# A third PSUM bank for the attention's transposes from tile 15 on, and the next step's decision two tiles earlier

## The reference

```
x = x + conv_attention(layernorm_over_channels(x))     # 7x7 local attention
t = tokens(x)                                          # 4 x 1024 x 64
t = t + steps(layernorm(t))
```

```
op = argmax(h[0, 0, :19])
q, k, v = h @ wq[op], h @ wk[op], h @ wv[op]
attn = softmax(q @ k.T / 8);  y = (attn @ v) @ wo[op]     # 1024 x 1024 per image
h = y if attn_mask[op] else h
z = relu(h @ w1[op] + b1[op]) @ w2[op] + b2[op]
h = z if ffn_mask[op] else h
```

## Time and profile before

| | |
|---|---|
| time, median of 3 runs | 262.25 us (262.2 to 262.34) |
| the profiled execution's own time | 261.88 us |
| its span in the trace | 260.0 us |
| TensorE busy (matmuls) | 230.6 us, 89% |
| VectorE busy | 170.7 us, 66% |
| ScalarE busy | 160.2 us, 62% |
| mean granted TensorE clock | 0.954 |

### The profile page before, as it was taken

The page is one execution under the profiler, slowest core; times in us unless marked ns, Lnnn a source line. Parts: engine busy times, 40 slices in busy tenths (PEclk is TensorE's granted clock), DMA queues, the critical chain, the costliest instruction groups (busy, mean ns, idle before and its releaser), DMA issues.

```text
span 260.0 us, 5251 instructions
## 1 busy us (share of the span) xinstructions
PE 230.6 (89%) x1794; PEld 156.5 (60%) x1795; DVE 170.7 (66%) x312; ACT 160.2 (62%) x297; POOL 39.5 (15%) x66
## 2 busy tenths in 40 slices
PE   7879963999999996499869999999999999998992
PEld 3247623787777744233247687887877777777320
DVE  0279937677778736146385999898687666871652
ACT  1928753366666784045456997879877776663541
POOL 9800042454444100700000000000000000000000
PEclk9999997799999996579989999999999999999999
DMA  6850000000000010000100000000000000000006
GB/s 167 186 108 1 4 0 1 0 3 0 0 0 0 0 31 0 10 0 3 43 0 0 3 0 0 3 0 3 0 3 0 3 0 3 0 3 0 0 16 149
DMA packets 3304, 4.80 MB, mean 18 GB/s; under 512 B 1041, under 2 KB 2257, under 8 KB 3282
## 3 DMA queue, kind: packets, MB, share of 16 engines
q1 hardware_dynamic: 2758, 3.86, 6.6%
q10 hardware_dynamic: 524, 0.64, 1.1%
HBM read 3.45 MB, written 1.05 MB: 17 GB/s over the span
## 4 chain that ended last, share of the span: by engine, by line
PE 75%; ACT 9%; DVE 7%; issue 6%; ACTq 2%; POOL 0%; DVEq 0%; POOLq 0%
PE ps L594 11%; PE ps L608 11%; PE ps L582 8%; PE ps L660 7%; PE ps L435 7%; PE ps L674 6%; PE ps L467 5%; PE ps L456 5%; ACT arena L883 4%; PE ps L446 2%; PE ps L410 2%; PE ps L334 2%; PE ps L563 2%; DVE arena L996 2%; PE ps L352 2%
## 5 line engine op out<-in xcount | busy, mean ns | idle before, releaser
L883 ACT COPY arena<-ps 128x1024 f32<-128x1024 f32 x32 | 32.4, 1011 | 20.4 <-PE ps L594 19.4
L582 PE MATMUL ps<-h_st,g_st 128*128 128x512 f32 x128 | 39.5, 431 | 2.6 <-DVE h_st L1094 2.3
L1107 DVE TENSOR_REDUCE negmax<-ps 128x1 f32<-128x1024 f32 x32 | 38.7, 1219 | 3.8 <-PE ps L582 3.6
L832 ACT ACTIVATE pr<-ps,negmax 128x1024 f32<-128x1024 f32 x32 | 35.8, 1119 | 4.0 <-DVE negmax L1107 3.7
L594 PE MATMUL ps<-eye,pr 128*128 128x128 f32 x256 | 33.7, 275 | 2.7 <-ACT arena L883 2.3
L594 PEld LDWEIGHTS ps<-eye,pr 128*128 128x128 f32 x256 | 28.6, 140 | 11.1 <-issue 5.0
L608 PE MATMUL ps<-arena,vk 128*64 128x128 f32 x512 | 31.5, 276 | 1.1 <-ACT arena L883 1.1
L608 PEld LDWEIGHTS ps<-arena,vk 128*64 128x64 f32 x512 | 27.6, 137 | 3.8 <-issue 2.3
L766 ACT ACTIVATE prob<-ps,negmax 128x308 f32<-128x308 f32 x32 | 16.3, 513 | 21.0 <-DVE negmax L1007 21.0
L582 PEld LDWEIGHTS ps<-h_st,g_st 128*128 128x128 f32 x128 | 22.2, 193 | 11.3 <-DVE h_st L1094 3.5
L1117 DVE TENSOR_SCALAR pr<-pr,rinv 128x1024 f32<-128x1024 f32 x32 | 24.1, 753 | 1.1
(11 more groups left out here) (110 smaller groups left out, 335.7 us busy)
## 6 DMA issues: line engine op xcount, KB each, us to landing
arena<-in_key_onehot SPq DMA_DIRECT2D x4, 361.0 KB, 6.2
out<-tabs SPq DMA_DIRECT2D x8, 128.0 KB, 2.3
x<-in_x SPq DMA_DIRECT2D x2, 256.0 KB, 3.9
x<-in_x ACTq DMA_DIRECT2D x2, 256.0 KB, 5.2
w1d<-in_ffn_w SPq DMA_DIRECT2D x4, 64.0 KB, 2.1
w2p<-in_ffn_pack SPq DMA_DIRECT2D x2, 65.5 KB, 1.9
spread_w<-in_spread_mat SPq DMA_DIRECT2D x4, 32.0 KB, 5.0
mean_w<-in_mean_mat SPq DMA_DIRECT2D x1, 96.0 KB, 2.1
```

The source lines that it names most:

```text
L582: mm = nc.tensor.matmul(ps[:, 2 * h + c, :], g_st[:, b2, h, q0:q0 + P], h_st[:, b2, h, part, c * 512:c * 512 + 512], start=(part == 0), st ...
L832: nc.scalar.activation(pr[:, n % 2, :], ps[:, 2 * (n % 2):2 * (n % 2) + 2, :], ACT.Exp, bias=negmax[:, 0, n % 2:n % 2 + 1], accum_out=rows ...
L883: nc.scalar.copy(prt[:, n // 8 % 2, n % 2, :, q0:q0 + P], ps[:, 4:6, :].rearrange("p b (c q) -> p (b c) q", c=4)).then_inc(S["s_pt"], 1)
L1107: nc.vector.tensor_reduce(negmax[:, 0, n % 2:n % 2 + 1], ps[:, 2 * (n % 2):2 * (n % 2) + 2, :], mybir.AxisListType.XY, ALU.max, negate=Tru ...
```

## The change

From tile 15 on (`RING`), an odd tile's transposes go to banks 5 and 6 and begin with bank 6, and an even tile's go to banks 4 and 5 and begin with bank 4. In both cases four transposes are issued before the wait for the copy of the previous tile, and four, into the shared bank 5, behind it. The ScalarE copy reads the two banks in their order. Since bank 6 also carries the row for the decision, `turn_row(6)` is issued at tile 12 and `decide` at tile 13, and `tile_turn(15)` waits for `decided`. Tiles 0 to 14 are transposed as before.

```diff
+RING = 15
...
                 def tile_turn(n):
                     pe.wait_ge(S["s_prob"], base + n + 1)
+                    bank, halves = 4, (0, 1)
                     if n == 0:
                         pe.wait_ge(S["vo_copied"], 3 * a + 1)
-                    else:
+                    elif n < RING:
                         pe.wait_ge(S["s_pt"], base + n)
-                    for c in range(NKC):
-                        mm = nc.tensor.transpose(ps[:, 4 + c // 4, (c % 4) * P:(c % 4) * P + P],
-                                                 pr[:, n % 2, c * P:c * P + P], eye[:])
+                    elif n % 2 == 1:
+                        bank, halves = 5, (1, 0)
+                    if n == RING:
+                        pe.wait_ge(S["decided"], a + f + 2)
+                    for i in halves:
+                        if n >= RING and i == halves[1]:
+                            pe.wait_ge(S["s_pt"], base + n)
+                        for c in range(4 * i, 4 * i + 4):
+                            mm = nc.tensor.transpose(ps[:, bank + i, (c % 4) * P:(c % 4) * P + P],
+                                                     pr[:, n % 2, c * P:c * P + P], eye[:])
                     mm.then_inc(S["s_turned"], 1)
...
-                    if n == 14:
+                    if n == 12:
                         pe.wait_ge(S["vo_copied"], 3 * a + 3)
                         pe.wait_ge(S["h_ready"], chunks + 5)
                         turn_row(6)
...
                     q0 = (n // 2 % 4) * P
+                    bank = 5 if n >= RING and n % 2 == 1 else 4
                     nc.scalar.copy(prt[:, n // 8 % 2, n % 2, :, q0:q0 + P],
-                                   ps[:, 4:6, :].rearrange("p b (c q) -> p (b c) q", c=4)
+                                   ps[:, bank:bank + 2, :].rearrange("p b (c q) -> p (b c) q", c=4)
                                    ).then_inc(S["s_pt"], 1)
...
-                           11: lambda: store(0), 15: lambda: decide(a + f + 1, 6, ev),
+                           11: lambda: store(0), 13: lambda: decide(a + f + 1, 6, ev),
```

## The result

The changed kernel took 258.73 us (median of 6 runs, 256.8 to 259.27) beside 261.88 us for the kernel before (6 runs, the three shown ahead among them); the ratio is 0.987 with a 95% interval of 0.9828 to 0.9912. In a second comparison the two came to 258.63 and 261.56 us, ratio 0.9907 (0.9878 to 0.9936). So it is about 3 us faster. The forecast was 258.9 us with a range of 258.3 to 260.3.

A forecast was written before the change was run, and what follows sets the result against it. TensorE's exposed waits for ScalarE's copy were taken to lie on the path; -3.6 for eight waits, +0.2 for late weight loads and +0.1 for a store made -3.3, from 262.25 to 258.9 us, range 258.3 to 260.3.

The forecast's parts named there:

- The bound: Attention tiles: TensorE's transposes wait for ScalarE's copy nine times, 2.3 us idle, on the path to the end.
- The waits that go: Odd tiles from 15 to 29: eight exposed waits for the copy vanish, 0.45 us each, 3.6 us together.
- The wait in the middle: Between an odd tile's fourth and fifth transposes: met by 0.02 us; late weight loads cost 0.2 us in all.
- What is late next: VectorE and ScalarE beside TensorE's 5.71 us pairs: their loop does not bind; a store costs 0.1 us.
- the loop over VectorE and ScalarE: Exponentials, normalising, maxima and copy of a tile pair: 5.51 us, 0.20 under TensorE's 5.71, so not binding.
- The 0.1 us for `store(1)`: VectorE's store after tile 19 delays tile 20's normalising: 0.1 us, bounds 0 and 0.3.
- The decision and its row: Row's transpose moved from tile 14 to 12, `decide` now earlier on VectorE: net 0, bounds -0.1 and +0.1.
- The sum: Whole kernel: -3.6 + 0.2 + 0.1 = -3.3 us, giving 258.9 us from the median of 262.25 us.
- A: Wait inside a run breaks overlap of weight loads; eight odd tiles pay 0.16 us each; 260.1 us; chance 0.16.
- B: VectorE and ScalarE become the bound, pairs of 5.9 us, gain only 2.1 us; 260.2 us; chance 0.10.
- C: Wait inside the run costs a full restart in all 17 tiles from 15 to 31; 262.9 us; chance 0.04.
- D: Second half still waits for the whole copy, early transposes only fill idle time; 262.2 us; chance 0.04.

The follow-up runs named there:

- e1: Kernel before with only the row's transpose moved to tile 12 and the decision to tile 13: stretch 64.38 us, median 261.58 us, ratio 0.9959.
- e4: Changed kernel with the wait for the previous tile's copy put ahead of the first four transposes: stretch 64.31 us, median 261.24 us, ratio 0.9962 to before.
- e5: Changed kernel plus one single-column ScalarE copy ahead of each even tile's copy from 16 on: stretch 61.00 us, median 258.08 us, ratio 0.9873 to before.
- e5b: Changed kernel plus two single-column ScalarE copies ahead of each even tile's copy from 16 on: stretch 61.66 us, median 258.92 us, ratio 0.9901 to before.
- e7: Changed kernel plus a VectorE memset ahead of each even tile's maxima from tile 15 on: stretch 63.16 us, median 260.57 us, ratio 0.9957 to before.
- e3: Kernel before plus an already met wait for the copy inside each run of transposes from tile 15 on: stretch 64.35 us, median 261.13 us, ratio 0.996.
- e10_last_shared: Kernel with three banks from tile 13 and ScalarE's key copies one tile earlier, plus tile 31's copy shared with VectorE: median 257.87 us, ratio 0.9861 to before.

## Why the prediction was right

- **The bound.** TensorE's waits for the copy, on the path, nine times: right, and by their stretches e1 and e4 show that nothing else in the change matters.
- **The waits that go.** 8 x 0.45 = 3.6 us; measured 3.65 us in the stretch. This term was the whole effect, and it came from setting an undisturbed pair beside a held-up one, not from the 2.3 us of the earlier trace rows, which has only the idle part.
- **The wait in the middle.** Forecast met by 0.02 us, with 0.2 us in all for late weight loads. Measured: met by about 0.06 us and no cost. The transposes of odd tiles take 1.03 to 1.04 us, as a run without the wait. The term was too large by 0.2. The 166 ns that the Trainium skill, "TensorE: Matmul & The Clock Gate", section "Single matmul latency", gives for a matmul by itself (it states it for bf16; these transposes are fp32) had nothing to act on: even an open wait in the middle (e5, e5b) cost at most 0.04 us beyond its lateness.
- **What is late next.** Not the loop over VectorE and ScalarE, as forecast: 5.36 us, 0.35 under TensorE's 5.71, where I had 0.2. The 0.1 us for `store(1)` did not appear: tile 20's transposes begin at 202.70 us on TensorE's timeline, 5.69 after tile 18's at 197.01. I had the wrong waiter: nearest to being late on VectorE was `mix(8)`, which waits for that store to free bank 7 and which no step of mine named. It was met, so the sum holds.
- **The decision and its row.** 0, measured 0.01 (e1).
- **The sum.** -3.3 forecast; the stretch says -3.65, the medians -3.15 and -2.93. The two small costs that I added were not there. That the medians come out below the stretch is not a sign of them: the runs of transposes and the pairs would show them, and the fifth mix's start varies by more. That 258.9 lies so near to the measured 258.73 is in part luck: it was worked out from a median of 262.25 us, and from the 261.88 of the six runs the same sum gives 258.6.
- **The rivals.** A is out by the lengths of the runs, B by the pairs of 5.71 us, though e7 shows that a longer instruction on VectorE would have brought it about, C by e3, D by the chain.

## What to carry to other kernels

Price an exposed wait by the period of an undisturbed repetition against a held-up one, not by the idle time alone: here 0.45 against 0.25 us. Where two engines take turns on one buffer, a third half-buffer lets the producer start before the consumer is done, and the wait belongs at the first write that needs the freed half. When the last wait of a kind goes, look at the next queue one pair later: with the ring from tile 13 one small copy on ScalarE took back most of it, and moving it and the three like it by one tile brought it in.

## What the runs showed of the hardware

- A met semaphore wait between two transposes on TensorE costs nothing measurable (17 of them, stretch 64.35 against 64.37 us).
- A weight load behind an open wait in the middle of a run started 0.05 us after the end of the copy that it waited for (211.13 to 211.18, and so in all seven such runs of e5b_copy_later), ahead of a run 0.12 us after it (199.06 to 199.18 in the earlier trace rows).
- ScalarE's copy of a single column is shown as 0.19 us, but the next copy starts 0.10 us after it (209.93, 210.03, 210.12 in e5b_copy_later).
- VectorE and ScalarE each copied 512 columns from neighbouring banks of PSUM at the same time in 0.69 and 0.59 us (e10_last_shared). Elsewhere in this section such a copy takes them 0.68 and 0.59 us.
